# State sums in two alternating accumulators, gate chain with one operand in PSUM, values of three head groups added in one bank, both orders sorted from new tables

## What is computed

```
s: x += ssm(ln(x))     xr = x W_in;  xc = silu(conv4(xr[:256]));  delta = softplus(xc)
                       h_n = exp(delta * A_n) * h_n + xc*xc   for 16 states n, along 512 tokens
                       y = xc * (sum_n h_n) * silu(xr[256:]) + D * xc;   out = y W_out
g: x += moe(ln(x))     r_e = |x - x Vg_e Vg_e'|,  rw = softmax(-r) over 8 experts
                       keep rw > 1/8 and among the two largest, normalize to w
                       out = sum_e w_e (x We_e + be_e) + x Wp + bp
t: x += attn(ln(x))    low-rank q, k, v, 16 heads of 8 features (+4 rotary), causal softmax, W_O
f: x += ffn(ln(x))     a = gated pair of 512, two dense 512x512 gelu layers, 512 -> 128
```

## Time and profile before

| | us |
|---|---|
| median of three runs | 1684.76 (1684.60 to 1685.74) |
| the profiled execution, first to last instruction | 1683.4 |

### The profile page before, as it was taken

One profiled execution on the slowest core, in us unless ns is written; L12 is line 12 of the kernel. 1 busy time (PEld: TensorE's weight loads), 2 busy tenths in 40 slices (PEclk: granted clock), 3 DMA queues, 4 the chain that ended last, 5 costly groups with the idle time before them and its releaser, 6 DMA issues.

```text
span 1683.4 us, 24214 instructions
## 1 busy us (share of the span) xinstructions
PE 1510.7 (90%) x7815; PEld 799.2 (47%) x7815; DVE 1401.6 (83%) x2550; ACT 1267.5 (75%) x2176; POOL 1251.9 (74%) x1211
## 2 busy tenths in 40 slices
PE   5256799999999999999999999998999899999997
PEld 2123244443444444444444344433444578888886
DVE  4899899999999999999999998998541477987773
ACT  5776798988989898898989898896646555555552
POOL 4988798988989898898989898898332345555553
PEclk8576999999999999999999999999999899999999
DMA  4000000000000000000000000000200000000000
GB/s 150 1 0 1 19 1 20 13 7 20 1 20 2 19 11 10 19 1 20 1 19 5 16 20 1 19 1 20 79 11 20 1 1 13 14 13 14 13 13 27
DMA packets 14686, 27.58 MB, mean 16 GB/s; under 512 B 3981, under 2 KB 4566, under 8 KB 14042
## 3 DMA queue, kind: packets, MB, share of 16 engines
q1 hardware_dynamic: 14554, 25.98, 5.5%
HBM read 9.20 MB, written 4.19 MB: 8 GB/s over the span
## 4 chain that ended last, share of the span: by engine, by line
PE 50%; POOL 20%; DVE 15%; ACT 7%; issue 7%; DMA 1%; SPq 0%; POOLq 0%; ACTq 0%; DVEq 0%
PE bank L1041 9%; POOL sum_fast L641 8%; PE bank L1523 7%; PE bank L1499 6%; DVE state_fast L623 5%; PE bank L695 5%; PE bank L1108 4%; PE bank L494 3%; POOL prob_fast L1091 3%; ACT prob_fast L1057 2%; PE bank L728 2%; POOL g_prod_fast L871 2%; PE bank L1543 2%; ACT state_fast L608 2%; PE bank L897 2%
## 5 line engine op out<-in xcount | busy, mean ns | idle before, releaser
L641 POOL TENSOR_TENSOR sum_fast<-sum_fast,state_fast 128x512 f32<-128x512 f32 x448 | 584.4, 1304 | 69.5 <-DVE state_fast L623 31.9
L623 DVE TENSOR_TENSOR_SCAN state_fast<-state_fast,bank 128x512 f32<-128x512 f32 x512 | 596.0, 1199 | 6.9 <-ACT state_fast L608 6.8
L1057 ACT ACTIVATE prob_fast<-bank 128x1024 f32<-128x1024 f32 x320 | 325.8, 1020 | 120.1 <-PE bank L1041 112.3
L1041 PE MATMUL bank<-stacks_fast 64*128 64x512 f32 (+3 forms) x2048 | 369.7, 470 | 18.3 <-ACT prob_fast L1057 11.8
L608 ACT ACTIVATE state_fast<-chan_all_kept,neg_a_fast 128x512 f32<-128x512 f32 x512 | 347.6, 714 | 10.2 <-POOL sum_fast L641 5.2
L1041 PEld LDWEIGHTS bank<-stacks_fast 64*128 64x128 f32 x2048 | 173.2, 188 | 241.2 <-ACT prob_fast L1057 106.9
L1091 POOL TENSOR_SCALAR_AFFINE_SELECT prob_fast<-prob_fast 128x512 f32<-128x512 f32 x256 | 167.7, 669 | 123.0 <-ACT prob_fast L1057 122.9
L1108 PE MATMUL bank<-prob_fast,v_ext_fast 128*32 128x512 f32 (+3 forms) x2048 | 182.4, 459 | 41.9 <-POOL prob_fast L1091 40.7
L1712 POOL TENSOR_TENSOR cell_a_fast<-th_fast,cell_a_fast 128x512 fp32r<-128x512 f32 x64 | 90.3, 1411 | 143.1 <-ACT cell_a_fast L1584 143.0
L728 PE MATMUL bank<-we_t_fast,xnt_g_fast 128*128 128x512 f32 x256 | 139.9, 640 | 2.8 <-DVE own_fast L858 1.0
L695 PE MATMUL bank<-resid_m_fast,xnt_g_fast 128*128 128x512 f32 x256 | 128.9, 616 | 10.2 <-DVE gate_fast L778 7.8
(11 more groups left out here) (214 smaller groups left out, 2664.5 us busy)
## 6 DMA issues: line engine op xcount, KB each, us to landing
stacks_fast<-parts_fast SPq DMA_DIRECT2D x128, 64.0 KB
stacks_fast<-rest_fast SPq DMA_DIRECT2D x128, 32.0 KB
out_x<-f_out_fast SPq DMA_DIRECT2D x16, 256.0 KB, 2.0
x_res_kept<-in_x SPq DMA_DIRECT2D x1, 2048.0 KB, 13.9
chan_all_kept<-in_h_t SPq DMA_DIRECT2D x2, 1024.0 KB, 7.9
x_res_kept<-in_x SPq DMA_DIRECT2D x1, 1024.0 KB, 9.5
chan_all_kept<-in_w_t SPq DMA_DIRECT2D x3, 256.0 KB, 2.9
x_res_kept<-in_x SPq DMA_DIRECT2D x2, 256.0 KB, 3.3
```

The lines of the kernel that those rows point to most:

```text
L623: dve.tensor_tensor_scan(h[:], h[:], self.banks[0][:], 0.0, ALU.mult, ALU.add).then_inc(self.v_scan.sem)
L641: pool.tensor_tensor(total[:], total[:], h[:], ALU.add).then_inc(self.p_sum.sem)
L1041: ins = pe.matmul(self.scores(b, step)[:, c:c + SEQ - P * kt], rows[:, 1, h // 2, P * kt:P * kt + P], rows[:, 0, h // 2, P * kt:SEQ], star ...
L1057: act.activation(self.probs[u % 2][:, i * 1024:(i + 1) * 1024], self.scores(b, 5 * g + n)[:], ACT.Exp, scale=SCALE).then_inc(self.a_prob.sem)
```

## The change

**State sums.** There are three accumulators now. The first sum adds states 0 and 1 into `sums[ct]`, the second states 2 and 3 into `sums[2]`, the others add one state to the two in turn, each waiting for the sum before the last, and the fifteenth adds the two. The count stays at 15 per half.

**Gate chain.** Part of the intermediate results lie in bank 4 (`sp`, `rwp`, `rank`, `kp`, `diff`), so that each DVE instruction with two tensor inputs has at most one in SBUF. The product `rw` is written twice, to SBUF and to PSUM. The guard is a maximum with a constant. The one long step is cut at each wait into 14 steps in all.

**Attention values.** Groups 0, 1 and 2 are added in bank 7 on top of each other: each uses a window of the same 32 rows, and the weights outside its 9 columns are zero. One copy, transposition, reciprocal and product serve the three, a second set group 3.

**Order.** All entries of TIMES and EDGES, PERIOD and F_PERIOD are new, in both phases. Six small weights share buffers with `num[1]` and `attn`; the first step of phase two waits for the second sequence's input too.

```diff
@@ act_decays
-                act.wait_ge(self.p_sum.sem, self.p_sum.at(bb, half * (STATE - 1) + max(nn - 1, 0)))
+                act.wait_ge(self.p_sum.sem, self.p_sum.at(bb, half * (STATE - 1) + (nn // 2 if nn < 4 else nn - 2)))
@@ pool_sums
-            total, h = self.sums[ct], self.state(b, i)
-            pool.wait_ge(self.v_scan.sem, self.v_scan.at(b, i))
...
+            total, other = self.sums[ct], self.sums[CT]
+            first = ct * (STATE - 1)
+            if n == 1 or n == 2:
+                i += n - 1
+                pool.wait_ge(self.v_scan.sem, self.v_scan.at(b, i))
...
+                pool.tensor_tensor((total, other)[n - 1][:], self.state(b, i - 1)[:], self.state(b, i)[:],
+                                   ALU.add).then_inc(self.p_sum.sem)
+            elif n < STATE - 1:
+                part = (total, other)[(n - 1) % 2]
+                pool.wait_ge(self.v_scan.sem, self.v_scan.at(b, i + 1))
+                pool.wait_ge(self.p_sum.sem, self.p_sum.at(b, first + n - 3))
+                pool.tensor_tensor(part[:], part[:], self.state(b, i + 1)[:], ALU.add).then_inc(self.p_sum.sem)
             else:
...
+                pool.wait_ge(self.p_sum.sem, self.p_sum.at(b, first + n - 2))
+                pool.tensor_tensor(total[:], total[:], other[:], ALU.add).then_inc(self.p_sum.sem)
@@ gate_room
+        sb, ps = self.gate, self.banks[4]
+        by_e = lambda at, i: at[:, i:i + NT * NE].rearrange("p (k e) -> p k e", k=NT)
+        return by_e(sb, 0), by_e(ps, 0), by_e(sb, 32), by_e(ps, 32), by_e(ps, 64), by_e(sb, 96), by_e(ps, 128)
@@ dve_g_gate
+        ss, sp, rw, rwp, rank, fw, kp = self.gate_room()
...
+        diff = self.banks[4][:, 256:512].rearrange("p (k e j) -> p k e j", k=NT, e=NE)
...
-        dve.tensor_tensor(rw, ss, over_e(col(2)), ALU.mult).then_inc(c.sem)
...
+        dve.tensor_tensor(rw, sp, over_e(col(2)), ALU.mult).then_inc(c.sem)
+        dve.tensor_tensor(rwp, sp, over_e(col(2)), ALU.mult).then_inc(c.sem)
+        yield
+        dve.wait_ge(c.sem, c.at(b, 3))
+        dve.tensor_tensor(diff, rwp.unsqueeze(2).to_broadcast([P, NT, NE, NE]),
                           rw.unsqueeze(3).to_broadcast([P, NT, NE, NE]), ALU.subtract).then_inc(c.sem)
...
-        dve.scalar_tensor_tensor(out=fw, in0=rw, scalar=thr, in1=rw, op0=ALU.is_gt, op1=ALU.mult).then_inc(c.sem)
+        dve.scalar_tensor_tensor(out=fw, in0=rwp, scalar=thr, in1=rw, op0=ALU.is_gt, op1=ALU.mult).then_inc(c.sem)
...
+        dve.scalar_tensor_tensor(out=kp, in0=rank, scalar=limit, in1=fw, op0=ALU.is_lt, op1=ALU.mult).then_inc(c.sem)
...
-        dve.scalar_tensor_tensor(out=col(4), in0=kept, scalar=0.0, in1=kept, op0=ALU.is_equal, op1=ALU.add).then_inc(c.sem)
...
+        dve.tensor_scalar(col(4), kept, KEPT_MIN, None, ALU.max).then_inc(c.sem)
@@ dve_t_proj
+        dve.tensor_scalar(slots[:, :, 0:7:3, 0:DH], from_v[:, :, 0:JOINT], 1.0, None, ALU.mult)
+        dve.tensor_scalar(slots[:, :, 7, 0:DH], from_v[:, :, JOINT], 1.0, None, ALU.mult).then_inc(self.v_t_val.sem)
@@ pe_values
+                        ins = pe.matmul(bank[32 * j:32 * j + 32, P * kt:SEQ], v_ext[:, v:v + 32],
+                                        self.probs[u % 2][:, c:c + SEQ - P * kt], start=(kt == 0 and g % JOINT == 0),
+                                        stop=(kt == 2 and g in ENDS), tile_position=(0, 32 * j), skip_group_check=True)
                 ins.then_inc(self.t_pv.sem)
...
+            if g not in ENDS:
+                continue
@@ dve_values
+        for i, n in enumerate((JOINT, GROUPS - JOINT)):
...
+            dve.reciprocal(rden[:, :, 0:n].unsqueeze(3), of[:, :, :, DH:DH + 1]).then_inc(self.v_rden.sem)
+            yield
+            dve.wait_ge(self.v_rden.sem, self.v_rden.at(b, i))
+            dve.tensor_tensor(to, of[:, :, :, 0:DH], rden[:, :, 0:n].unsqueeze(3).to_broadcast([P, NT * GROUP, n, DH]),
                               ALU.mult).then_inc(self.v_attn.sem)
```

More of the change, by code:

```diff
@@ L340, in phase_one_room @@
         self.rest = [sb(f"rest{i}", [ROPE_ROWS, SEQ]) for i in range(2)]
-        self.v_ext = [sb(f"v_ext{i}", [P, NT, HEADS * VW + 32 - VW]) for i in range(2)]
+        self.v_ext = [sb(f"v_ext{i}", [P, NT * GROUP * V_UNIT + 32 - VW]) for i in range(2)]
         self.stacks = sb("stacks", [P, 2, PAIRS, SEQ])
@@ L746, in act_g_gate @@
         act, banks = self.act, self.banks
[L747 removed]
+        ss, sp = self.gate_room()[0:2]
         yield
@@ L1061, in act_nums @@
         act = self.act
-        for g in range(GROUPS):
+        for i, g in enumerate(ENDS):
             yield
             act.wait_ge(self.t_pv.sem, self.t_pv.at(b, 3 * g + 2))
-            if g > 1:
-                act.wait_ge(self.t_num.sem, self.t_num.at(b, g - 2))
-            elif b and g == 1:
-                act.wait_ge(self.t_num.sem, self.t_num.at(b - 1, 3))
+            if b and i:
+                act.wait_ge(self.t_num.sem, self.t_num.at(b - 1, 1))
             elif b:
                 act.wait_ge(self.t_t_out.sem, self.t_t_out.at(b - 1))
-            act.activation(self.num[g % 2][:], self.banks[7][:], ACT.Copy).then_inc(self.a_num.sem)
+            act.activation(self.num[i][:], self.banks[7][:], ACT.Copy).then_inc(self.a_num.sem)
         yield
         act.wait_ge(self.t_back.sem, self.t_back.at(b))
-        act.wait_ge(self.t_num.sem, self.t_num.at(b, 2))
+        act.wait_ge(self.t_num.sem, self.t_num.at(b, 0))
         act.activation(self.num[0][:], self.banks[2][:], ACT.Copy).then_inc(self.a_back.sem)
@@ L1099, in pe_values @@
                 yield
-                if kind == 0 and b + g:
-                    pe.wait_ge(self.v_attn.sem, self.v_attn.at(b, g - 1))
+                if kind == 0 and g % JOINT == 0 and b + g:
+                    pe.wait_ge(self.v_attn.sem, self.v_attn.at(b, g // JOINT - 1))
                 if g + kind == 0:
@@ L1169, in rooms_in_turn @@
             self.states = [sb(f"state{i}", [P, SEQ]) for i in range(STATE_BUFFERS)]
-            self.sums = [sb(f"sum{i}", [P, SEQ]) for i in range(CT)]
+            self.sums = [sb(f"sum{i}", [P, SEQ]) for i in range(CT + 1)]
         sb = self.room(area, tag, "right")
@@ L1316, in pool_setup @@
         for v in self.v_ext:
-            pool.memset(v[:], 1.0)
+            pool.memset(v[:], 0.0).then_inc(self.p_zeros.sem)
+        for i, v in enumerate(self.v_ext):
+            pool.wait_ge(self.p_zeros.sem, self.p_zeros.at(0, i))
+            for g in range(GROUPS):
+                pool.memset(self.v_slots(v)[:, :, V_SLOT[g], DH:VW], 1.0)
         if not general:
@@ L1323, in pool_setup @@
             pool.memset(self.squares[:].bitcast(F32), 0.0).then_inc(done.sem)
-        pool.memset(self.gate[:, 64:100], 1.0).then_inc(done.sem)
+        pool.memset(self.gate[:, 128:164], 1.0).then_inc(done.sem)
     def act_f_rstd(self, b):
@@ L1842, in layouts @@
     head, rot = by_pair(DH), by_pair(DR)
+    across = np.arange(HEADS * DH).reshape(GROUPS, GROUP, DH).transpose(1, 0, 2).reshape(-1)
     g = {
```

383 lines of the change are left out of this document (195 added, 188 removed).

## The result

The change takes the median from 1685.25 us (1684.60 to 1688.89) to **1607.22 us** (1605.50 to 1609.73), a ratio of 0.9528 (95% interval 0.9511 to 0.9545). I had said 1648, with 1626 to 1676 as range. The sign was right; the gain is 78 us where I expected 37, and lies outside the range.

What follows compares the result with a forecast made beforehand. Taken to bound the kernel: 12 middle turns, held by a circle through PE's mask wait. Gains of 33.0 (turn 74.25 to 71.5), 3.5 and 1 us, 37.5 in all, gave 1648 us, range 1626 to 1676.

Steps and rivals of the forecast that it cites:

- The circle over PE's wait for the mask: Middle turns: mask wait, late scores, late masks; wait costs PE 2.23 us per turn, plus about 1.6 where clock falls.
- the 0.7 of them: Middle stretch: PE's clock falls to half in about 0.7 of the turns, costing about 1.6 us there.
- The terms: Work per turn after the change: PE 67.7, DVE 67.2, ACT 66.0, POOL 66.7 us with 2.4 less in gaps.
- a pitch: POOL's neighbouring sums start 1.22 us apart instead of 1.42, taking 2.4 us of gaps off each turn.
- L723's slack: Gate weights on PE: the gate chain ends at 635.1, PE gets there at 636.7, slack 1.6 us.
- head: First 277 us, with half-clock stretches and setup: a gain of 1 us, bounds -4 to +5.
- The new maximum: DVE gate chain: L826 as a maximum with a constant falls from 1124 to 161 ns, 0.96 us; the uncertain term.
- its 4% over the fullest: Middle turn: if it stays 4% longer than the fullest engine's work, it takes 70.4 to 70.9 us.
- 69.7, is too good: Middle turn with the whole mask wait also gone, 69.7 us: rejected, as three engines would be over 96% full.
- 71.5: Forecast middle turn in us, from 74.25, chosen nearer to 71.9, where PE keeps all 4.2 us of idle time.
- The rivals: Maximum stays blocked 1654, 0.12; wait only moves 1666, 0.22; parts inactive 1674, 0.06; gaps close 1629, 0.10; slower 1693, 0.06.
- All gaps close: Rival for the middle turns: turn 70.0 us, gain 55 us, time 1629 us; chance 0.10.

Runs made afterwards that it cites:

- e3: Kernel before with POOL's last two masks of group 3 moved ahead of later sums; 1658.57 us, ratio 0.9831.
- e12: Kernel before with only the alternating sum accumulators, old order, plus shared weight buffers and phase two's added wait; 1656.40 us, ratio 0.9826.
- e10: Kernel before with only the new gate chain, old order, plus shared weight buffers and phase two's added wait; 1687.46 us, ratio 1.0002.
- e11: Kernel before with only the new attention values, old order, plus shared weight buffers and phase two's added wait; 1689.67 us, ratio 1.0022.
- e5: Kernel after with the gate chain's intermediate results in SBUF again, steps and order unchanged; 1641.79 us, ratio 0.9719 to the kernel before.
- e1: Kernel after with the order tables of the kernel before, so new code in the old order; 1649.48 us, ratio 0.9774 to the kernel before.
- e9: e1 with POOL's masks steps 10 and 11 moved ahead of sums 20 and 21; 1640.53 us, ratio 0.9738 to the kernel before.
- e13: e9 with two DVE steps (third expert product, last pair of values) moved behind scans; 1651.03 us, ratio 0.9789 to the kernel before.
- e4: Kernel after with the old sums (one accumulator, each waiting for the one before), order unchanged; 1617.71 us, ratio 0.9587 to the kernel before.
- e7: Kernel after with each of a turn's eight value transposes on PE done twice; 1614.23 us, ratio 0.9563 to the kernel before.

## Why the prediction was wrong

- **What bounds the kernel: right, but not used.** The circle over PE's wait for the mask was there: e3 breaks it by place, e12 by POOL's time. The sum didn't use it, and went by the fullest engine in busy time. (The clock fell in 10 of the 12 turns, more than the 0.7 of them that I had worked out from means.)
- **The terms: right in sum.** PE's work fell from 69.6 to 67.2 (I had 67.7), DVE's from 69.8 to 66.7 (67.2), a block of four sums takes 4.94 us, a pitch of (4.94 - 1.27)/3 = 1.22, L723's slack 1.47 (1.6). After the twelfth turn 3.5 (3.5), head 4.1 (1), phase two 1.6 (0). For DVE errors cancel. Alone in the old order the gate chain takes 1.82 us off DVE and the values 0.19 (e10, e11), where I had 2.43 and 0.64; in the new order e5 puts 2.58 back. One mis-sized item is the reciprocal of 48 elements, 0.44 us where I had put 0.27 (the kernel after, by shapes):

```profile
L1190 DVE RECIPROCAL rden_fast<-bank 128x48 f32<-128x48 f32 x16 | 7.0, 437 | 20.1 <-PE bank L1155 20.1
```

- **The new maximum: right, but by its place.** L858 is short in the kernel after. That it can be blocked is shown by e10, where it stands elsewhere against POOL. In e1 it takes 169 to 170 ns in every execution, but another maximum with a constant is long there, the clamp at the head of the chain (L794 before). In ns shortest/median/longest, the maximum after and in e10, then the clamp in e1:

```profile
L858 DVE TENSOR_SCALAR gate_fast<-kept_all_kept x16: 170/171/1287, 121.5 to 1147.3; 128x4 f32<-128x4 f32 x16
```

```profile
L863 DVE TENSOR_SCALAR gate_fast<-kept_all_kept x16: 170/782/1024, 127.0 to 1222.2; 128x4 f32<-128x4 f32 x16
```

```profile
L830 DVE TENSOR_SCALAR gate_fast<-gate_fast x16: 153/1105/1689, 121.2 to 1184.6; 128x32 f32<-128x32 f32 x16
```

- **The failed step: from the work to the turn.** "If the turn keeps its 4% over the fullest", then "69.7, is too good: three engines would be over 96% full", then 71.5 "because filling gets harder as the engines draw level". Measured are 68.74 us with PE at 97.8%. The step treats idle time as a share that full engines must keep. It isn't one: it is the sum of waits at named places, and the order sets these places. Of the 2.76 us that my turn was too long, 0.5 are work (67.7 against 67.2) and 2.3 are idle time (3.8 against 1.51). Of PE's 4.63 us idle, 3.1 went, more than the mask's 2.23. That e1 in the old order comes to 71.70 doesn't support my 71.5: I had reached it with the mask moved, which e1 leaves where it was.
- **Each part counted once, whatever the order.** I gave the edits one price. They have two: in the old order, with its wait for the mask, only POOL's edit counts; in the new order, without that wait, the others count for more. The prices of a part range from less than nothing (e11 is 0.54 us per turn longer) to 3.95 us for the values, 0 to 2.40 for the gate, 0.47 to 2.38 for the sums.
- **The rivals.** None held it. "All gaps close" (70.0, 1629) was the nearest, and still left PE 2.3 us idle over its 67.7.
- **Open.** Which moves of the new order are worth the 2.38 us per turn between e9 and the kernel after. The one that I picked (e13) was not it, and a table of one engine can't be exchanged alone, since the lists would then wait for each other in a ring (this is argued; no run shows it). Open too is the head, which ends 3 us earlier than I had; no run looks at it.

## What to carry to other kernels

In a pipeline of in-order lists, find the loop of waits that sets the turn, and ask of each edit which step of that loop it shortens; work taken off elsewhere came back here as waits (e10, e11). Before calling an engine the fullest, add the gaps between its dependent instructions to its busy time (e4). When order and work change together, price the waits place by place in the new order and don't scale idle time with the fullest engine; with the places open, let the range reach down to the work of the fullest engine (67.7 here, 1648 - 12 x 3.8 = 1602). Test a part in both orders before calling it worthless.

## What the chip showed that I had not expected

- **One-input instructions are blocked as well, and whether they are is a matter of phase.** The same maximum of 4 elements per row took 170 ns in the median of the kernel after and 782 in e10, and the clamp over 32 elements 1105 in the median of e1, 1689 at most. The chain's two-tensor instructions over 32 elements with one operand in PSUM lay between 178 and 199 ns in every execution of e1 and e10. The Trainium skill, "SBUF — State Buffer", section "Who interferes with whom", says that such one-input forms can contend with GpSimd. These rows agree; in e10 it costs the maximum 0.61 us per turn, and in the kernel after the phase spares it.
- **The same holds with both tensors in SBUF.** In e5 three instructions of the chain over 32 elements have medians of 1198 to 1297 ns, and two others, with as many operands in SBUF, 191 and 192.
- **The time blocked doesn't follow the size.** In e5 an instruction over 32 elements takes between 177 and 1300 ns, 1.12 us more at the longest, less than one of POOL's sums lasts (1.27 us). That it waits for the end of POOL's instruction would fit, but e1's clamp takes up to 1.54 us more than its shortest, which is longer than one sum; no run separates it.
- **A reciprocal grows faster with its size than a product.** On DVE from PSUM, 16 elements take 0.25 us and 48 take 0.44, 5.8 ns an element; the products beside them go from 0.292 (128) to 0.558 (384), 1.04 ns an element.
- **Four busy lists can close to within 1.5 us of the fullest** (98.3% of PE in e7), with the granted clock at 1.00 through 825 us.
